# Expert output scattered straight to token order by row numbers carried with the rows, with the second batch's slots behind the first one's return

## The chip, the cores and the metric

The kernel runs on one core of one Trainium2 chip. The metric is the time of one execution on the device, in microseconds (us); lower is better.

## The reference

A network of four residual blocks works on x of shape (2, 1024, 128) in float32. Cut to what matters here:

```python
x = x + attention(layernorm(x))        # 16 heads of 64, both batches
x = x + routed_ffn(layernorm(x))       # the block that the change touches
x = x + ssm(layernorm(x))              # fc1, in_proj, causal conv, selective scan, fc2
x = x + dense_experts(layernorm(x))    # 8 experts, all computed

def routed_ffn(x):                     # 8 experts, 128 -> 512 -> 128
    logits = (x @ wg_red.T) @ wg_unit.T
    e, score = argmax(softmax(logits)), max(softmax(logits))
    h = gelu(x @ w1[e] + b1[e])
    return score * (h @ w2[e] + b2[e])
```

Each token goes to one expert only. The kernel computes the routed block with the tokens sorted by expert.

## The kernel before, in words

One list of steps (`whole_order`, built of `attention_order`, `routed_order`, `first_inputs_order`, `recurrence_order` and `dense_order`) sets the program. Each engine (and SP, which issues most DMAs) walks this list and takes the steps that its own table has; on an engine everything runs in that order, and between engines semaphores set the pace. So a step that waits holds back all later steps of its engine.

**Routing.** A batch has 1024 tokens in 8 tiles of 128. `dve_count` (L1687 on) gives each token a place, so that every expert's tokens begin at a new slot of 128 rows; 15 slots (NSLOT) always do. `pool_scatter` (L2097) writes the 8 tiles of normed rows (`K.xrows`, 128 floats a row) to these places in the HBM tensor `slots_in`, two indirect DMAs to each of four steps. `load_rows` (L1444) loads four slots at once into one of two buffers `slot_rows`; SP issues it for batch 0, ACT for batch 1. Then for each group of four slots PE transposes (`turn`, L770) and ACT copies (`turned`, L1202).

**Slots.** For slot n: SP fetches the expert's weights (`fetch`, 578 KB), PE multiplies (`up`, L783), ACT applies gelu (L1214), PE multiplies again (`down`, L794), DVE adds the bias into one of six buffers `e0_y` (`yrow`, L1732), and SP stores them as slot n of the HBM tensor `slots_out` (L2283). Batch 0 has slots 0 to 14, batch 1 slots 15 to 29 (written s = 15, s + 1, ... below). The first hidden buffers hT share their memory with `slot_rows`.

**Return.** When all 15 slots of a batch are stored, POOL issues 8 gathers (`pool_back`, L2114), each of which brings the 128 rows of one tile in token order. For batch 0, DVE weighs each tile and adds it to x (`return`, L1744 and L1745), then come the layer norm's moments (`lnvar`), POOL's root (`lnroot`, L2031 and L2034) and the normed rows (`lnrows`, L1540), PE's transposes (`lnturn`, L593), and with them the third block: `fc1` (L809), `inp` (L819), 8 convolution taps on DVE (`conv`, L1772 and L1775), silu, `xpj` (L871), `dtp` (L892). For batch 1 the 8 gathers stand beside the units 0 to 7 of the recurrence, ACT weighs (`rescale`, L1178) and PE adds (`readd`, L827 and L829).

**The order around the change.** In `routed_order`, after slot 14 of batch 0: row loads of batch 1, the 8 gathers of batch 0, then batch 1's four `turn`s, the `up`s of s to s + 5 and the `down`s of s to s + 3, while the gathers and the layer norm run; `first_inputs_order` weaves the other slots among the third block's first products.

**Recurrence.** 64 units, each: PE spreads B (L909), DVE multiplies (L1852) and scans (L1859), POOL multiplies with C (L2181), PE adds (L925), ACT makes the decay (L1340).

Of the kernel before, what the change touches and what calls it, by code (L numbers as in the profile page):

```python
# [167 lines left out]
class Names:  # L168
# [7 lines left out]
         (4, 0, 3): [("lnturn", 1, 0), ("lncopy", 1, 0)], (4, 0, 5): [("lnturn", 1, 1), ("lncopy", 1, 1)], (5, 0, 3): [("bias", 1)], (2, 0, 5): [("gdir",)],  # L176
# [147 lines left out]
def routed_order():  # L324


    s, beside = NSLOT, {3: [("lnrows", 3)], 4: turned(3), 8: [("scatter", 1, q) for q in range(4)] + [("fetch", NSLOT)], 10: [("fetch", NSLOT + 1)], 12: [("fetch", NSLOT + 2)]}
# [8 lines left out]
    order += [("rows", 1, 0), ("rows", 1, 1)] + [("back", 0, t) for t in range(NT)] + [("fetch", s + 3)]  # L336
    order += [("turn", 1, 0), ("turned", 1, 0), ("rows", 1, 2), ("fetch", s + 4), ("up", s), ("gelu", s), ("turn", 1, 1), ("turned", 1, 1), ("rows", 1, 3)]
    order += [("up", s + 1), ("gelu", s + 1), ("down", s), ("turn", 1, 2), ("turned", 1, 2)]
    order += [("fetch", s + 5), ("up", s + 2), ("gelu", s + 2), ("down", s + 1), ("turn", 1, 3), ("turned", 1, 3)]
    order += [("up", s + 3), ("gelu", s + 3), ("down", s + 2), ("up", s + 4), ("gelu", s + 4), ("down", s + 3), ("up", s + 5), ("gelu", s + 5)]  # L340
    order += [("return", 0, t) for t in range(5)] + [("yrow", s), ("fetch", s + 6), ("return", 0, 5), ("yrow", s + 1), ("fetch", s + 7)]
    order += [("return", 0, 6), ("return", 0, 7), ("lnvar", 4), ("lnroot", 4), ("yrow", s + 2), ("fetch", s + 8)]
    return order + [("lnrows", 4), ("yrow", s + 3), ("fetch", s + 9)]


def first_inputs_order():

# [415 lines left out]
def pe_turn(K, pe, b, g):  # L763
# [5 lines left out]
    for t in range(n):  # L769
        ins = pe.transpose(bank[:, t * P:(t + 1) * P], R.slot_rows[i % 2][:, t, :], K.ident[:, :])  # L770
# [401 lines left out]
def act_rescale(K, act, t):  # L1172
# [4 lines left out]
    act.wait_ge(K.back[t], 16)  # L1177
# [27 lines left out]
def act_gelu(K, act, n):  # L1205
# [3 lines left out]
    act.wait_ge(R.ld_wts[BUFFER[n]], 16 * (USE[n] + 1))  # L1209
    users = [i for i in range(n) if HIDDEN[i] == HIDDEN[n]]  # L1210
# [233 lines left out]
def load_rows(K, eng, b, g):  # L1444
# [281 lines left out]

def dve_yrow(K, dve, n):
# [8 lines left out]
def dve_return(K, dve, b, t):  # L1736
# [3 lines left out]
    dve.wait_ge(K.back[t], 16)  # L1740
# [219 lines left out]
def dve_added(K, dve, b, c):  # L1960
# [7 lines left out]
    for t in range(4):  # L1968
        tt = 4 * c + t
        xs = K.x[:, b * NT + tt, :]  # L1970
        if last and t == 2:
# [9 lines left out]
             "rate": dve_rate, "count": dve_count, "yrow": dve_yrow, "return": dve_return, "conv": dve_conv, "xpj_take": dve_xpj_take, "xdr": dve_xdr,  # L1981
# [217 lines left out]
POOL_STEPS = {"full": pool_low, "firstroot": pool_first_root, "halfroot": pool_half_root, "xdr": pool_xdr, "dt": pool_dt, "du": pool_du, "centre": pool_centre, "gated": pool_gated, "fc2bias": pool_fc2_bias, "xlo": pool_xlo, "lnroot": pool_root, "e1_root": pool_root1, "score": pool_score, "scatter": pool_scatter, "back": pool_back, "pad": pool_pad,  # L2199
# [12 lines left out]
def sp_first_loads(K, sp):  # L2212
# [24 lines left out]
    for b in range(B):  # L2237
        sp.dma_start(R.slots_in[b].rearrange("(j p) d -> p j d", p=P), R.zero[:, :].unsqueeze(1).broadcast_to([P, NSLOT, D])).then_inc(
# [104 lines left out]
SP_STEPS = {"row": sp_row, "rows": sp_rows, "fetch": sp_fetch, "yrow": sp_yrow, "loads": sp_loads, "e1_load": sp_load_experts,  # L2343
# [11 lines left out]
def two_layer_program(nc, a, out):  # L2355
    K, A, R, X, Y = Names(), Names(), Names(), Names(), Names()
    K.A, K.R, K.X, K.Y, K.a, K.out = A, R, X, Y, a, out
    with ExitStack() as ctx:
# [37 lines left out]
        K.back, K.stored, K.returned, K.scored = sems("row_returned", AT), sem("stored"), sem("returned"), sem("scored")  # L2396
# [210 lines left out]
```

## Time and profile before

| what | value |
|---|---|
| median of 3 runs | 1140.87 us (1140.73 to 1142.6) |
| the profiled execution's own time | 1139.21 us |
| its span | 1137.9 us, 19726 instructions |
| busy: PE, DVE, ACT, POOL | 96%, 73%, 54%, 67% of the span |
| DMA queue of POOL (q0) | 1024 packets, 2.10 MB |

How to read it: the attention takes the time to about 711 us, batch 0's slots to 745 us, the return, batch 1's slots and the third block's first products to 803 us, the recurrence to about 1030 us, and the dense experts the rest. Shares of the whole span say nothing of these stages; the stretch between 733 and 860 us is where the change acts.

### The profile page before, as it was taken

The numbers are of one execution on the slowest core, as the hardware profiler recorded it, in microseconds if no ns is written. First come the engines' busy times: TensorE is split into PE (matmuls) and PEld (weight loads), VectorE is DVE, ScalarE is ACT, GpSimd is POOL, SyncE is SP. The second block draws the span as 40 slices with busy tenths as digits, with TensorE's granted clock in tenths as the row PEclk, the third lists the DMA queues.
The fourth block names the chain that finished last, engine by engine and source line by source line (L and its number), as shares of the span: only waits on it lengthen the run. The fifth ranks groups of instructions, "written<-read, shape, count | busy, mean of one in ns | idle before, by whom it ended". The sixth has DMA issues, their size and how long they took to land.

```text
span 1137.9 us, 19726 instructions
## 1 busy us (share of the span) xinstructions
PE 1088.3 (96%) x7578; PEld 675.5 (59%) x7578; DVE 829.3 (73%) x1226; ACT 618.1 (54%) x866; POOL 761.0 (67%) x394
## 2 busy tenths in 40 slices
PE   7999999999999999999999999969789987899998
PEld 4555665665665665666566566967444434445786
DVE  6875766675775775676876547425889999997987
ACT  5543544553543554554354445546977555757653
POOL 5787788788787797677889850230589796995200
PEclk9999999999999999999999999989899999999999
DMA  6000000000000000000000333475464454440000
GB/s 210 1 3 1 1 2 1 1 2 2 1 2 2 1 1 2 2 1 1 2 11 6 97 113 105 121 233 168 159 204 155 142 164 140 140 158 28 10 10 19
DMA packets 38094, 68.86 MB, mean 61 GB/s; under 512 B 5969, under 2 KB 24145, under 8 KB 38001
## 3 DMA queue, kind: packets, MB, share of 16 engines
q1 hardware_dynamic: 34992, 64.52, 18.0%
q0 software_dynamic: 1024, 2.10, 0.6%
q8 instruction: 61, 1.00, 0.4%
q10 hardware_dynamic: 1984, 0.98, 0.3%
q14 instruction: 33, 0.26, 0.1%
HBM read 61.30 MB, written 6.16 MB: 59 GB/s over the span
## 4 chain that ended last, share of the span: by engine, by line
PE 79%; issue 7%; DVE 5%; POOL 5%; ACT 2%; DMA 1%; POOLq 0%; DVEq 0%; ACTq 0%
PE psum L651 20%; PE psum L612 16%; PE psum L637 6%; PE psum L625 5%; PE psum L669 5%; PE psum L1019 4%; PE psum L925 3%; PE psum L1002 3%; POOL hc L2181 3%; PE psum L717 3%; PE psum L703 3%; PE psum L684 2%; PE psum L794 2%; PE psum L783 1%; DVE psum L1852 1%
## 5 line engine op out<-in xcount | busy, mean ns | idle before, releaser
L2093 POOL TENSOR_TENSOR psums<-psums,prob 128x1024 f32<-128x1024 f32 x180 | 427.7, 2376 | 26.1 <-POOL psums L2093 0.5
L1568 DVE TENSOR_REDUCE mx<-psum 128x2 f32<-128x1024 f32 x256 | 300.8, 1225 | 116.5 <-PE psum L637 116.0
L1118 ACT ACTIVATE prob<-psum 128x1024 f32<-128x1024 f32 x256 | 261.5, 1027 | 64.5 <-PE psum L625 39.8
L651 PE MATMUL psum<-prob,V 128*64 128x512 f32 x1024 | 244.0, 598 | 0.0
L2181 POOL TENSOR_TENSOR hc<-hs,cc 128x1024 f32<-128x1024 f32 x64 | 151.7, 2371 | 21.1 <-DVE hs L1859 18.5
L1859 DVE TENSOR_TENSOR_SCAN hs<-dA,psum 128x1024 f32<-128x1024 f32 x64 | 146.3, 2286 | 2.2
L2093 POOL TENSOR_TENSOR psums<-prob 128x1024 f32<-128x1024 f32 x30 | 72.2, 2406 | 105.3 <-ACT prob L1118 105.3
L1127 ACT COPY oraw<-psum 128x512 f32<-128x512 f32 x32 | 18.8, 588 | 210.8 <-PE psum L651 210.8
L925 PE MATMUL psum<-hc,ident 128*128 128x512 f32 x256 | 122.6, 602 | 2.5 <-DVE slot_rows_h L1867 1.4
L651 PEld LDWEIGHTS psum<-prob,V 128*64 128x64 f32 x1024 | 66.5, 137 | 97.1 <-issue 93.2
L637 PE MATMUL psum<-k_hi,q_hi 64*128 64x512 f32 x512 | 107.7, 410 | 1.7 <-DVE mx L1568 1.3
L612 PE MATMUL psum<-q_hi,k_hi 64*128 64x512 f32 x512 | 106.9, 404 | 0.0
L612 PE MATMUL psum<-q_hi,k_lo 64*128 64x512 f32 x512 | 103.5, 390 | 0.0
L612 PE MATMUL psum<-q_lo,k_hi 64*128 64x512 f32 x512 | 103.3, 390 | 0.0
L625 PE MATMUL psum<-guard,row_one 64*128 64x512 f32 x512 | 103.1, 388 | 0.0
L1627 DVE SCALAR_TENSOR_TENSOR x<-psum,inv,x 128x128 f32<-128x128 f32 x256 | 72.0, 344 | 21.1 <-PE psum L717 15.6
L925 PEld LDWEIGHTS psum<-hc,ident 128*128 128x128 f32 x256 | 48.3, 192 | 44.5 <-issue 32.2
L637 PEld LDWEIGHTS psum<-k_hi,q_hi 64*128 64x128 f32 x512 | 50.3, 184 | 40.3 <-issue 28.0
L909 PE MATMUL psum<-xdr,pickr 128*128 128x512 f32 x128 | 57.1, 528 | 11.9 <-DVE hs L1859 11.6
L612 PEld LDWEIGHTS psum<-q_hi,k_hi 64*128 64x128 f32 x512 | 48.8, 184 | 33.0 <-ACT prob L1118 17.5
L1340 ACT ACTIVATE dA<-slotT,alog 128x1024 f32<-128x1024 f32 x32 | 36.6, 1150 | 40.0 <-DVE hs L1859 39.7
L625 PEld LDWEIGHTS psum<-guard,row_one 64*128 64x128 f32 x512 | 50.8, 184 | 8.7
(294 smaller groups left out, 1709.0 us busy)
## 6 DMA issues: line engine op xcount, KB each, us to landing
cc<-C_rows SPq DMA_DIRECT2D x64, 512.0 KB, 3.7
kq_wts<-in_e_rows SPq DMA_DIRECT2D x14, 578.0 KB, 5.0
e_wts<-in_e_rows SPq DMA_DIRECT2D x10, 578.0 KB, 3.9
e_w<-in_e_rows SPq DMA_DIRECT2D x6, 578.0 KB, 4.3
slots_in<-e_zero SPq DMA_DIRECT2D x2, 960.0 KB, 7.0
slots_out<-e_y SPq DMA_DIRECT2D x30, 64.0 KB, 2.6
e_w<-in_e_w SPq DMA_DIRECT2D x1, 1024.0 KB, 7.5
slot_rows_h<-slots_in SPq DMA_DIRECT2D x3, 256.0 KB, 2.9
```

The costliest lines, as they stand in the source:

```text
L612: pe.matmul(both[:, s, :], left[HALF[s], js], right[HALF[s], cs], start=(part == 0), stop=False)
L625: ins = pe.matmul(both[:, s, :], A.row_one[HALF[s], :], A.guard[q][HALF[s], cs], start=False, stop=True)
L637: ins = pe.matmul(both[:, s, :], A.q_hi[r][HALF[s], t * P:(t + 1) * P], A.k_hi[r][HALF[s], c * CH:(c + 1) * CH], start=True, stop=True)
L651: ins = pe.matmul(A.O[HALF[s], :], A.V[pair % 2][:, j, s * DH:(s + 1) * DH], A.prob[unit(pair, c, j) % NPB][:, s * CH:(s + 1) * CH], start ...
L909: ins = pe.matmul(X.gain[u % 2][:, c * CH:(c + 1) * CH], X.pickr[:, n:n + 1].broadcast_to([P, P]), X.xdr[b][:, c * CH:(c + 1) * CH], start ...
L925: ins = pe.matmul(X.Y[:, c * CH:(c + 1) * CH], K.ident[:, :], X.hc[u % 3][:, c * CH:(c + 1) * CH], start=(u > 0 and n == 0), stop=(n == NS ...
L1118: act.activation(A.prob[n % NPB][:, :], slots.bank("score", pair, c, j).rearrange("p s n -> p (s n)"), ACT.Exp, scale=float(DH) ** -0.5).t ...
L1568: dve.tensor_reduce(K.A.mx[:, :, t, c], slots.bank("max", pair, t, c), AXX, ALU.max).then_inc(*slots.inc("max", pair, t, c))
L1627: ins = dve.scalar_tensor_tensor(out=K.x[:, tile, :], in0=slots.bank("out", pair, c)[:, s, t * P:(t + 1) * P], scalar=A.inv[:, s * NT + 4 ...
L1859: dve.tensor_tensor_scan(X.hs[u % 3][:, :], X.dA[u % 3][:, :], X.gain[u % 2], 0.0, ALU.mult, ALU.add).then_inc(X.state_done, 1)
L2093: pool.tensor_tensor(total[:, :], (K.A.prob[(n - 1) % NPB] if j == 1 else total)[:, :], K.A.prob[n % NPB][:, :], ALU.add).then_inc(*K.psum ...
L2181: pool.tensor_tensor(X.hc[u % 3][:, :], X.hs[u % 3][:, :], X.cc[u % NCC][:, :], ALU.mult).then_inc(X.product_done, 1)
```

## The change

- Every row of `xrows` gets a 129th float. Once, early, DVE writes into it the number at which the token's output row shall stand (`names`): NSLOT * P + token. Two DMAs (`pads`, on SP, beside attention pair 6) write the numbers 0 to 1919 into the 129th column of `slots_in`, for rows that no token takes. So each slot row carries its token's number, and the padding rows carry numbers below 1920.
- DVE copies that column of four loaded slots into an integer tile (`tokens`, one short copy for each group of four slots). A row load waits until the copy of the group that had its buffer before is made.
- The store of a slot on SP goes; POOL scatters the slot's rows to `rows_out` by these numbers (`pool_yrow`): 15 indirect DMAs a batch in place of 8 gathers.
- The gathers go; SP loads the token rows in order, two plain loads of 256 KB a batch (`sp_back`), when all 15 scatters of the batch have landed.
- The order is written anew: batch 0's return, its moments and `lnrows` stand ahead of batch 1's row loads and slots. Batch 1's last scatter step comes behind slot 14. Ahead of `lnturn` of the third block now stand two `turn`s, two `up`s and one `down`; the others come behind.

```diff
-    s, beside = NSLOT, {3: [("lnrows", 3)], 4: turned(3), 8: [("scatter", 1, q) for q in range(4)] + [("fetch", NSLOT)], 10: [("fetch", NSLOT + 1)], 12: [("fetch", NSLOT + 2)]}
+    s, beside = NSLOT, {3: [("lnrows", 3)], 4: turned(3), 8: [("scatter", 1, 0), ("fetch", NSLOT)], 9: [("scatter", 1, 1)], 10: [("fetch", NSLOT + 1)], 12: [("scatter", 1, 2), ("fetch", NSLOT + 2)]}
...
-    order += [("rows", 1, 0), ("rows", 1, 1)] + [("back", 0, t) for t in range(NT)] + [("fetch", s + 3)]
-    order += [("turn", 1, 0), ("turned", 1, 0), ("rows", 1, 2), ("fetch", s + 4), ("up", s), ("gelu", s), ("turn", 1, 1), ("turned", 1, 1), ("rows", 1, 3)]
-    order += [("up", s + 1), ("gelu", s + 1), ("down", s), ("turn", 1, 2), ("turned", 1, 2)]
-    order += [("fetch", s + 5), ("up", s + 2), ("gelu", s + 2), ("down", s + 1), ("turn", 1, 3), ("turned", 1, 3)]
-    order += [("up", s + 3), ("gelu", s + 3), ("down", s + 2), ("up", s + 4), ("gelu", s + 4), ("down", s + 3), ("up", s + 5), ("gelu", s + 5)]
-    order += [("return", 0, t) for t in range(5)] + [("yrow", s), ("fetch", s + 6), ("return", 0, 5), ("yrow", s + 1), ("fetch", s + 7)]
-    order += [("return", 0, 6), ("return", 0, 7), ("lnvar", 4), ("lnroot", 4), ("yrow", s + 2), ("fetch", s + 8)]
-    return order + [("lnrows", 4), ("yrow", s + 3), ("fetch", s + 9)]
+    order += [("scatter", 1, 3), ("back", 0)] + [("return", 0, t) for t in range(NT)] + [("lnvar", 4), ("lnroot", 4), ("lnrows", 4)]
+    order += [("rows", 1, 0), ("rows", 1, 1), ("fetch", s + 3)]
+    order += [("turn", 1, 0), ("turned", 1, 0), ("tokens", 1, 0), ("tokens", 1, 1), ("rows", 1, 2), ("fetch", s + 4), ("up", s), ("gelu", s), ("turn", 1, 1), ("turned", 1, 1), ("rows", 1, 3)]
+    order += [("up", s + 1), ("gelu", s + 1), ("down", s), ("yrow", s)] + turned(4)
+    order += [("turn", 1, 2), ("turned", 1, 2), ("tokens", 1, 2), ("fetch", s + 5), ("up", s + 2), ("gelu", s + 2), ("down", s + 1), ("yrow", s + 1), ("fetch", s + 6)]
+    return order + [("fc1", 0), ("fc1_out", 0), ("turn", 1, 3), ("turned", 1, 3), ("tokens", 1, 3), ("up", s + 3), ("gelu", s + 3), ("down", s + 2), ("yrow", s + 2), ("fetch", s + 7)]
...
+    order = [("inp", 0, 0), ("inp_out", 0, 0), ("up", s + 4), ("gelu", s + 4), ("down", s + 3), ("yrow", s + 3), ("fetch", s + 8)]
+    order += [("inp", 0, 1), ("inp_out", 0, 1), ("up", s + 5), ("gelu", s + 5), ("down", s + 4), ("yrow", s + 4), ("fetch", s + 9)]
     for i in range(4):
         order += [("conv", 0, i // 2, w) for w in (i % 2 * 2, i % 2 * 2 + 1)]
+        order += [("up", s + 6 + i), ("gelu", s + 6 + i), ("down", s + 5 + i), ("yrow", s + 5 + i), ("fetch", s + 10 + i)]
...
-        beside[t] += [("back", 1, t)]
+        beside[t] += [("back", 1)] * (t == 0)
...
 def load_rows(K, eng, b, g):
...
     if i >= 2:
         eng.wait_ge(*K.work.full.at("turn", *divmod(i - 2, 4)))
+        eng.wait_ge(R.tokens, i - 1)
...
+def dve_tokens(K, dve, b, g):
+    R, i = K.R, b * 4 + g
+    n = min(4, NSLOT - 4 * g)
+    dve.wait_ge(R.ld_rows[i % 2], 16 * (i // 2 + 1))
+    dve.tensor_copy(R.tok[b][:, 4 * g:4 * g + n], R.slot_rows[i % 2][:, 0:n, D]).then_inc(R.tokens, 1)
...
+def pool_yrow(K, pool, n):
+    R = K.R
+    b, j = divmod(n, NSLOT)
+    pool.wait_ge(R.tokens, 4 * b + j // 4 + 1)
+    pool.wait_ge(*K.work.empty("down", n))
+    pool.indirect_dma_start(out=R.rows_out[b], out_offset=bass.IndirectOffsetOnAxis(ap=R.tok[b][:, j:j + 1].bitcast(U32), axis=0),
+                            in_=R.yrow[n % NY][:, :], in_offset=None).then_inc(R.y_stored[n % NY], 16)
...
+def sp_pads(K, sp):
+    R = K.R
+    sp.wait_ge(R.named, 1)
+    for b in range(B):
+        sp.dma_start(R.slots_in[b].rearrange("(j p) d -> p j d", p=P)[:, :, D], R.pad[:, :], allow_slow_non_contiguous=True).then_inc(R.padded, 16)
...
+def sp_back(K, sp, b):
+    R = K.R
+    sp.wait_ge(R.scattered[b], 16 * NT)
+    for i in range(NY):
+        sp.wait_ge(R.y_stored[i], 16 * len(range(i, (b + 1) * NSLOT, NY)))
+    for g in range(NC):
+        at = slice(b * NT + 4 * g, b * NT + 4 * g + 4)
+        sp.dma_start(K.xrows[:, at, :], R.rows_out[b][NSLOT * P + g * CH:NSLOT * P + (g + 1) * CH, :].rearrange("(t p) d -> p t d", p=P)).then_inc(K.back[b * NC + g], 16)
```

## Rows read from the trace of the kernel before

**Rows 1.** Busy time of stretches: PE, PEld, DVE, ACT, POOL, then PEclk, DMA share, GB/s

```profile
0.00:570.00 570.00, 564.13 (x4761) 342.99 (x4763) 391.76 (x616) 279.41 (x322) 440.10 (x213) 1.00 0.04 12
...
745.00:769.40 24.40, 13.79 (x96) 12.98 (x95) 7.01 (x33) 9.68 (x30) 9.60 (x10) 0.86 0.76 228
769.40:802.80 33.40, 33.05 (x197) 25.66 (x198) 18.08 (x31) 25.46 (x56) 0.00 (x0) 0.95 0.47 142
808.00:860.00 52.00, 45.62 (x115) 22.14 (x116) 47.43 (x30) 44.20 (x91) 44.34 (x31) 0.91 0.58 194
860.00:1000.00 140.00, 126.86 (x347) 61.31 (x346) 137.86 (x98) 88.05 (x103) 122.91 (x61) 1.00 0.46 147
```

**Rows 2.** Chain that ended last, around batch 0's return: start, length, what

```profile
745.41 3.98 DMA slots_out<-e_y
...
759.11 5.45 DMA xrows<-slots_out,posi
```

**Rows 3.** Timeline of PE: start, length, engine, line, instruction, count, idle before it

```profile
750.23 1.12 PE L770 MATMUL psum<-ident,slot_rows_h 128*128 128x128 f32 x4 [5.18 <-DMA slot_rows_h<-slots_in]
...
757.25 0.60 PE L770 MATMUL psum<-ident,slot_rows_h 128*128 128x128 f32 x4
...
769.44 0.74 PE L593 MATMUL psum<-ident,xrows 128*128 128x128 f32 x4 [3.76 <-DVE xrows L1540]
...
781.02 1.06 PE L794 MATMUL psum<-kq_wts,slot_rows_h 128*128 128x128 f32 x8
781.91 1.06 PE L783 MATMUL psum<-slotT,kq_wts 128*128 128x128 f32 x8
...
802.56 1.42 PE L909 MATMUL psum<-xdr,pickr 128*128 128x512 f32 x4
```

**Rows 4.** Timeline of POOL

```profile
733.35 0.96 POOL L2104 DMA_INDIRECT slots_in<-xrows,posi  x1 [0.30 <-issue]
...
740.93 0.96 POOL L2104 DMA_INDIRECT slots_in<-xrows,posi  x1 [0.30 <-issue]
...
766.56 1.68 POOL L2034 TENSOR_TENSOR rstd<-std,exponent 128x8 f32<-128x8 f32 x1
...
812.05 1.09 POOL L2114 DMA_INDIRECT xrows<-slots_out,posi  x1 [0.17 <-POOL hc L2181]
```

**Rows 5.** Timeline of DVE

```profile
733.06 0.49 DVE L1732 TENSOR_TENSOR e_y<-psum,kq_wts 128x128 f32<-128x128 f32 x2
...
757.45 0.29 DVE L1744 BATCH_NORM_STATS2 stats<-x 128x6 f32<-128x128 f32 x1 [1.03 <-DMA xrows<-slots_out,posi]
...
758.09 0.29 DVE L1744 BATCH_NORM_STATS2 stats<-x 128x6 f32<-128x128 f32 x1
...
764.79 0.34 DVE L1745 SCALAR_TENSOR_TENSOR x<-xrows,score,x 128x128 f32<-128x128 f32 x1
...
768.27 2.13 DVE L1540 TENSOR_SCALAR xrows<-x,mv,rstd 128x128 f32<-128x128 f32 x8 [1.96 <-POOL rstd L2034]
...
779.23 0.81 DVE L1772 TENSOR_SCALAR u<-xc,cw,cb 128x1024 f32<-128x1024 f32 x1 [2.94 <-ACT xc L1232]
...
787.28 2.60 DVE L1775 SCALAR_TENSOR_TENSOR u<-xc,cw,u 128x1024 f32<-128x1024 f32 x2
```

**Rows 6.** DMA issues of the page: KB each, median us from issue to landing

```profile
slot_rows_h<-slots_in SPq DMA_DIRECT2D x3, 256.0 KB, 2.9
slot_rows_h<-slots_in ACTq DMA_DIRECT2D x3, 256.0 KB, 4.3
...
slots_in<-xrows,posi POOLq DMA_INDIRECT x16, 2.2
```

**Rows 7.** Timeline of ACT, one gelu of a slot

```profile
754.15 1.14 ACT L1214 ACTIVATE slot_rows_h<-psum,e_wts 128x128 f32<-128x128 f32 x4 [2.18 <-PE psum L783]
```

**Rows 8.** Who waited for whom, 808 to 860 us: us in total, times, longest

```profile
DVE psum L1852 <- PE psum L909: 4.1, 4, 2.4
...
ACT xrows L1178 <- DMA xrows<-slots_out,posi: 2.8, 2, 1.7
```

More of the change, by code:

```diff
@@ L175 @@
 EARLY = {(3, 0, 3): [("lnvar", 1), ("lnroot", 1)], (3, 1, 3): [("lnrows", 1)],
-         (4, 0, 3): [("lnturn", 1, 0), ("lncopy", 1, 0)], (4, 0, 5): [("lnturn", 1, 1), ("lncopy", 1, 1)], (5, 0, 3): [("bias", 1)], (2, 0, 5): [("gdir",)],
+         (4, 0, 3): [("lnturn", 1, 0), ("lncopy", 1, 0)], (4, 0, 5): [("lnturn", 1, 1), ("lncopy", 1, 1)], (5, 0, 3): [("bias", 1)], (6, 0, 5): [("pads",)], (2, 0, 5): [("gdir",), ("names",)],
          (8, 1, 3): [("lnvar", 2), ("lnroot", 2)], (9, 0, 3): [("lnrows", 2)],
@@ L357, in first_inputs_order @@
-    order += [("xpj", 0), ("xpj_take", 0), ("gelu", s + 11), ("gelu", s + 12), ("pick",), ("up", s + 13), ("up", s + 14), ("dtp", 0, 0), ("xpj_out", 0)]
-    order += [("gelu", s + 13), ("gelu", s + 14), ("xdr", 0), ("dtp_out", 0, 0), ("softexp", 0, 0), ("down", s + 11), ("yrow", s + 11), ("dtp", 0, 1), ("dtp_max",)]
+        order += [("up", s + 6 + i), ("gelu", s + 6 + i), ("down", s + 5 + i), ("yrow", s + 5 + i), ("fetch", s + 10 + i)]
+    order += [("silu", 0, 0), ("up", s + 10), ("down", s + 9), ("silu", 0, 1), ("up", s + 11), ("yrow", s + 9), ("fetch", s + 14)]
@@ L359, in first_inputs_order @@
+    order += [("xpj", 0), ("xpj_take", 0), ("gelu", s + 10), ("gelu", s + 11), ("pick",), ("up", s + 12), ("dtp", 0, 0), ("xpj_out", 0), ("down", s + 10), ("yrow", s + 10)]
+    order += [("up", s + 13), ("gelu", s + 12), ("gelu", s + 13), ("xdr", 0), ("dtp_out", 0, 0), ("down", s + 11), ("yrow", s + 11), ("up", s + 14), ("gelu", s + 14), ("softexp", 0, 0), ("dtp", 0, 1), ("dtp_max",)]
     for n in range(s + 12, s + 15):
@@ L1209, in act_gelu @@
     act.wait_ge(R.ld_wts[BUFFER[n]], 16 * (USE[n] + 1))
+    if HIDDEN[n] < 2:
+        act.wait_ge(R.tokens, 4 * B)
     users = [i for i in range(n) if HIDDEN[i] == HIDDEN[n]]
@@ L1739, in dve_return @@
     t += b * NT
-    dve.wait_ge(K.back[t], 16)
+    dve.wait_ge(K.back[t // 4], 16)
     if t > b * NT:
@@ L1980 @@
              "rowed": dve_row, "valued": dve_values, "sumhalf": dve_sum_half, "out": dve_out, "gsum": dve_gate_squares, "gscale": dve_gate_scale, "gdir": dve_gdir, "choose": dve_choose,
-             "rate": dve_rate, "count": dve_count, "yrow": dve_yrow, "return": dve_return, "conv": dve_conv, "xpj_take": dve_xpj_take, "xdr": dve_xdr,
+             "names": dve_names, "tokens": dve_tokens, "rate": dve_rate, "count": dve_count, "yrow": dve_yrow, "return": dve_return, "conv": dve_conv, "xpj_take": dve_xpj_take, "xdr": dve_xdr,
              "dtp_out": dve_dtp_first, "dtp_max": dve_dtp_max, "dt": dve_dt, "gain0": dve_gain0, "pick": dve_pick, "alog": dve_alog, "unit": dve_unit, "output": dve_output,
@@ L2340, in sp_added @@
     sp.dma_start(K.out.rearrange("(t p) d -> p t d", p=P)[:, at, :], K.x[:, at, :]).then_inc(K.stored, 16)
-SP_STEPS = {"row": sp_row, "rows": sp_rows, "fetch": sp_fetch, "yrow": sp_yrow, "loads": sp_loads, "e1_load": sp_load_experts,
+SP_STEPS = {"row": sp_row, "pads": sp_pads, "rows": sp_rows, "fetch": sp_fetch, "back": sp_back, "loads": sp_loads, "e1_load": sp_load_experts,
             "xpj_out": sp_store_C, "unit": sp_unit, "added": sp_added}
```

65 lines of the change are left out of this document (31 added, 34 removed).

## The prediction

> **What bounds the kernel now.** I first cut the span into stretches by busy time. Between 745.0 and 769.4 us no engine is full: PE works 13.79 of 24.40 us, DVE 7.01, POOL 9.60 [rows 1]. The chain of waits says why: the last slot's store has to land (3.98 us), then 8 gathers follow each other on POOL, and the last one lands 5.45 us after its issue [rows 2]. The timeline of DVE shows the last tile added at 764.79 and the normed rows ready at 768.27 + 2.13 = 770.40; PE's first `lnturn` starts at 769.44 [rows 3, 5]. PE uses this wait for batch 1: four `turn`s, six `up`s and four `down`s stand between 750.2 and 765.7. From there to the recurrence PE is the bound: 33.05 of 33.40 us busy [rows 1], ending with L909 at 802.56 [rows 3]. In the recurrence DVE is: 137.86 of 140 us from 860 on, but only 47.43 of 52 in its first part, 808 to 860 [rows 1]. So time is to be had in two places, the wait of 24 us and DVE's 4.57 idle us; anything added to PE between 769 and 803 us is paid in full.
>
> **Step 1, POOL's queue.** The 15 stores of batch 0 leave SP and become indirect DMAs on POOL, among the 8 scatters of batch 1. Seven scatters in a row start at 733.35 to 740.93, so one takes 7.58 / 6 = 1.26 us of POOL [rows 4]. Slots come every 1.79 us (an `up` and a `down` of 0.89 each, the distance of 781.02 and 781.91 [rows 3]), so slots alone would fit; slots and scatters together don't. DVE finishes slots 6 and 7 between 733.06 and 733.55, together, as it was in the routing sums of batch 1 before [rows 5]. From 733.6 POOL has, in its order: y6, y7, 2 scatters, y8, 2 scatters, y9, y10, y11, 2 scatters, y12, y13, y14. y14 is the 15th, so it starts at 733.6 + 14 x 1.26 = 751.3, although its rows are made at 745.4. Before, the SP store of it started at 745.4.
>
> **Step 2, the return.** A scatter lands 2.2 us after its issue begins [rows 6]: 753.5. SP then issues two loads of 256 KB. The same size and row length took 2.9 us from SP in a quiet stretch and 4.3 us from ACT in a busy one [rows 6]. No weight fetch runs beside these two (the next one waits for PE's `turn`), so I take 2.9 and 0.2 for the issue: first tile at 756.6. DVE takes 0.64 us a tile where it does not wait (757.45 to 758.09 [rows 5]), so the eighth is added from 756.8 + 7 x 0.64 = 761.3, against 764.79: 3.5 us earlier. From there to the last normed row it was 770.40 - 764.79 = 5.6 us, moments, POOL's root (1.68 us [rows 4]) and `lnrows`, and no scatter is left on POOL then (the last two start at 752.6 and 753.8). New end of `lnrows`: 766.9.
>
> The Trainium skill (DMA: Bandwidth & Descriptors, "Anatomy of one DMA — SWDGE (gpsimd) path") gives 2.0 us plus bytes over 436 GB/s, an estimate of 2.6 us for 256 KB; by it the return would be 0.3 us earlier than by my row.
>
> **Step 3, a new wait on ACT.** ACT's load of rows (1,2) now waits for `tokens` (1,0). In the list that copy stands on DVE behind `lnrows`, and behind the load on ACT stands gelu s; PE's `down` s waits for gelu s, and `lnturn` is queued behind `down` s. So after 766.9: the copy (0.3 at most, a 128 x 128 add is 0.25 each [rows 5]), gelu 1.14 [rows 7], `down` 0.89, hand-overs 0.3: 769.5. At half clock `down` takes 0.9 more: 770.4. I take 769.9, which is 0.5 us **later** than the 769.44 of before, though the rows came back 3.5 us earlier. Batch 1's row loads (issued at about 756.2, landing by 760.5 at 4.3 us) are ready long before and decide nothing.
>
> **Step 4, work moved behind.** Ahead of `lnturn` PE now does two `turn`s, two `up`s, one `down`; before, four, six and four. Behind it come 4 `up`s and 3 `down`s more, 7 x 0.89 = 6.2 us, and two `turn`s, 0.60 (four slots [rows 3]) and some 0.48 (three): 7.3 us. PE has 0.35 us free in the stretch [rows 1], so nothing hides it: +7.3. The half clock at the stretch's start (0.95 mean [rows 1]) stays about as it is.
>
> **Step 5, the convolution.** The taps with four bias adds between them took DVE from 779.23 to 787.28 + 2.60 = 789.88, 10.65 us [rows 5]. They now stand behind `yrow` s + 4, so behind `down` s + 4, at about 785.3, and end at about 795.9; PE has work until about 795.2 by the sum so far, and `xpj` needs the second half of the silus some 1.8 us into itself. Late by 0 to 1 us; I take +0.3.
>
> **Step 6, the recurrence.** Eight gathers leave POOL (1.09 us and a gap of 0.17 beside each product [rows 4]), and ACT no longer waits 2.8 us for them [rows 8]. DVE waited for PE's L909 4.1 us in four places [rows 8]; each follows from `readd`, a silu or a transposition which ACT or POOL made late. I take all 4.1 back; bounds are 0 (PE and ACT in order keep them) and 4.57. After 860 DVE is full, so this gain stays. The second batch's `back` lands behind unit 0 and is first needed at unit 2.
>
> **Costed at nothing.** `names` and four `tokens` beside the attention: some 0.3 us each on a DVE with 391.76 of 570 us busy [rows 1]. SP loses its stores and gets `back`, behind which the fetches of s + 3 and on queue; they wait for `turn`s anyway and their slots come later than before. The six `e0_y` buffers: a scatter issued at 739.9 or so has landed when slot 14 needs its buffer; if not, DVE and PE would stop some 1 us. POOL's last three scatters of batch 1 end at about 812.5, its first `du` is then due at 813.5: cover 1 us. `pads`: DMA share there is 0.04 [rows 1]; uncovered it would hold SP's guard rows of one pair. The Trainium skill (same page, "Rules for kernel authors") says that a non-contiguous last dimension becomes one descriptor per element, so 2 x 1920; no row here shows such a transfer. Rows of 129 floats in place of 128 are 0.8% more bytes; at worst a row load is later by 1.4 us, the distance of the two kinds of load [rows 6], and those loads decide nothing.
>
> **Sum.** +0.5 + 7.3 + 0.3 - 4.1 = **+4.0 us**. The profiled execution took 1139.21 us (span 1137.9), so its like would be 1143.2; the median of the runs is 1.66 above it: 1140.87 + 4.0 = **1144.9 us**.
>
> **Rivals.**
> - *The return is early enough, not slower.* If POOL's descriptors overlapped its gaps so that y14 went out when made, at 745.7, steps 2 and 3 would come 5.6 us earlier: 4.0 - 5.6 = -1.6, 1139.3. It decides as soon as one indirect DMA costs POOL under about 0.9 us. Against it: seven at 1.26 without exception [rows 4]. With it, and DVE's last 0.5 idle us back too, 1138.8. A milder one: half of that, 1142.
> - *The recurrence gives nothing back.* ACT is busy 44.20 of 52 us there and reloads tables, PE 45.62 [rows 1]; if the four waits stay, +8.1: 1149.0. For it: only 2.8 us are waits for gathers. Against it: each wait lies behind one of them.
> - *TensorE cold for longer.* The granted clock was 0.86 over the wait [rows 1]: after 5.18 idle us the same transposes took 1.12 us, at 757.25 only 0.60 [rows 3], the two levels of 1.2 and 2.4 GHz. Now PE idles from 745 to 760 and works in pieces to 770. If it stays at the lower level for 4 us more from 770 on, half of them is lost: +6.0, 1146.9. The Trainium skill (TensorE: Matmul & The Clock Gate, "Part 1") says that the half-rate state is the default and activity releases it; the trace agrees.
> - *The burst of fetches.* Behind `turn` (1,2) ten fetches go out at once, and scatters share the DMA engines (0.76 busy in the wait already [rows 1]): if y scatters and row loads land 2 us later each, +2 to +4, 1147 to 1149.
> - *`pads` stalls attention*: one guard row late by 5.45 us, the slowest landing shown [rows 2]: 1150.3.
>
> **How the numbers follow.** Two runs of this kernel differ by about 0.2%, 2.3 us: faster is under 1138.6, slower over 1143.2. Forecast as worked out (+2.3 to +6): 0.48. Early return 0.18, of which 0.10 passes under 1138.6; step 3 or 4 shorter than summed (0 to +2.3) 0.16; nothing given back 0.05, cold clock 0.06, burst 0.05, pads 0.02. Faster 0.10, same 0.08 + 0.16 = 0.24, slower 0.48 + 0.18 = 0.66. Range 1139.8 to 1149.5.
>
> **What would show it.** Right: y14's scatter starts near 751; last return near 761; gelu s right behind the `tokens` copy, near 767; `lnturn` near 770; L909 of unit 0 near 810.5 (802.56 before); DVE's waits for L909 under 1 us up to unit 12. Wrong: y14 before 748, `lnturn` before 766, or PE idle behind `lnturn`.

## The result and the profile after

The changed kernel took 1146.73 us (median of 7 runs, 1146.28 to 1148.21) against 1142.6 us of the kernel before in the same session (7 runs, 1140.73 to 1145.37): a ratio of 1.0039, 95% interval 1.0027 to 1.0052, so 3.1 to 5.9 us slower. The forecast was slower by 4.0 us.

The profiled execution after took 1146.28 us, its span was 1144.9. Its busy time by stretch (columns as in [rows 1]):

```profile
745.00:769.40 24.40, 8.79 (x44) 8.04 (x45) 6.27 (x28) 4.48 (x15) 9.97 (x11) 0.64 0.27 74
769.40:810.00 40.60, 38.34 (x254) 31.27 (x253) 17.24 (x36) 28.45 (x75) 12.28 (x12) 0.96 0.60 211
810.00:860.00 50.00, 41.85 (x130) 21.52 (x129) 47.66 (x37) 47.65 (x89) 35.87 (x21) 0.93 0.58 199
```

PE worked 8.79 us of the wait for batch 0's rows, where it had worked 13.79 [rows 1]. Some of the 8.79 is batch 0's last slots, late in this execution; in the second profile below PE works 6.35 us of the same stretch. What the prediction doesn't have stands in the chain that ended last, before that wait:

```profile
735.83 0.91 PE psum L791 x8
736.80 7.62 another core or an unknown queue
744.47 2.88 another core or an unknown queue
...
755.74 2.24 DMA rows_out<-e_y,e_wg
758.16 3.74 DMA xrows<-rows_out
```

PE, ACT and DVE stood still in turn between 737 and 754 us (called "the stop" below), and no instruction that the profile shows released them; POOL went on issuing an indirect DMA every 1.26 us until 743.27. Slot 14's rows were made at 754.69, 9.3 us later than in the next profile when both are counted from the same event, and its scatter began at 755.74, not at 751.3. One profile can't say whether the change does this, so the kernel was profiled again (run look_after, under "The experiments"), and the second profile shows nothing of it. It is the one to read the steps from. Line numbers are those of each kernel's own file: `turn`, `up`, `down`, `lnturn`, `fc1` and the spread of B, L770, L783, L794, L593, L809 and L909 before, are L767, L780, L791, L590, L806 and L906 here.

POOL, DVE, ACT and PE of this second profile (span 1142.9, 1144.18 us), in four views (timelines, columns as in [rows 3 to 5]); first POOL:

```profile
734.79 0.96 POOL L2134 DMA_INDIRECT rows_out<-e_y,e_wg  x1 [4.75 <-DVE e_y L1750]
...
752.50 0.96 POOL L2134 DMA_INDIRECT rows_out<-e_y,e_wg  x1 [0.30 <-issue]
```

That is y6 and y14, with 13 indirect DMAs between them: 17.71 / 14 = 1.265 us each, although slot 14's rows were made 6.7 us before their turn:

```profile
745.77 0.29 DVE L1750 TENSOR_TENSOR e_y<-psum,e_wts 128x128 f32<-128x128 f32 x1 [1.21 <-PE psum L791]
758.74 0.35 DVE L1763 SCALAR_TENSOR_TENSOR x<-xrows,score,x 128x128 f32<-128x128 f32 x1 [12.67 <-DMA xrows<-rows_out]
...
763.31 0.34 DVE L1763 SCALAR_TENSOR_TENSOR x<-xrows,score,x 128x128 f32<-128x128 f32 x1
...
766.77 2.14 DVE L1540 TENSOR_SCALAR xrows<-x,mv,rstd 128x128 f32<-128x128 f32 x8 [2.13 <-POOL rstd L2052]
768.83 0.23 DVE L1742 CAST e_wg<-slot_rows_h 128x4 int32<-128x4 f32 x2
```

The rows are all added at 763.31 instead of 764.79 [rows 5]; the last line is the two `tokens` copies, 0.23 us together, right behind `lnrows`. ACT, whose gelu s waits behind the row load that needs these copies:

```profile
769.59 0.63 ACT L1213 ACTIVATE slot_rows_h<-psum,e_wts 128x128 f32<-128x128 f32 x2 [5.29 <-DVE e_wg L1742]
```

PE, where `down` s (L791) waits for this gelu, and `lnturn` (L590) and `turn` (1,2) (L767) stand behind `down` s:

```profile
766.24 1.06 PE L767 MATMUL psum<-ident,slot_rows_h 128*128 128x128 f32 x4
767.09 1.80 PE L780 MATMUL psum<-slotT,e_wts 128*128 128x128 f32 x8
770.79 1.16 PE L791 MATMUL psum<-e_wts,slot_rows_h 128*128 128x128 f32 x8 [1.89 <-ACT slot_rows_h L1213]
771.78 1.64 PE L590 MATMUL psum<-ident,xrows 128*128 128x128 f32 x8
773.21 1.07 PE L767 MATMUL psum<-ident,slot_rows_h 128*128 128x128 f32 x4
```

The granted clock was at its lower level (0.50) up to 768.6, while PE had worked since 762.57, and at its upper level (1.00) from 768.7 to 772.0, so `down` s took only 0.99 us to the next start. Behind the gap of 1.89 us it was at 0.50 again from 772.1 to 775.4: `turn` (1,2) took 1.07 us, like the `turn` at 766.24.

And who waited for whom between 808 and 860 us, where DVE had waited 4.1 us for L909 [rows 8]:

```profile
DVE psum L1870 <- PE psum L906: 0.3, 1, 0.3
```

### The profile page after: what moved, and what is told of

It is laid out like the page before. It is cut to its first block, busy times and chain, and to the rows that moved or that the text cites. A ratio compares the mean times of both kernels' runs of the same rounds, so it can differ in the third digit from the quotient of the medians.

```text
span 1144.9 us, 19769 instructions
## 1 busy us (share of the span) xinstructions
PE 1088.9 (95%) x7578; PEld 676.0 (59%) x7578; DVE 836.1 (73%) x1237; ACT 617.7 (54%) x866; POOL 775.3 (68%) x408
## 4 chain that ended last, share of the span: by engine, by line
PE 74%; issue 9%; DVE 7%; ACT 4%; POOL 3%; DMA 1%; another core or an unknown queue 1%; SPq 0%; DVEq 0%; POOLq 0%; ACTq 0%
PE psum L648 20%; PE psum L609 16%; PE psum L634 6%; PE psum L622 5%; PE psum L666 5%; PE psum L1016 3%; PE psum L999 3%; DVE psum L1870 3%; PE psum L714 3%; PE psum L700 2%; PE psum L681 2%; POOL hc L2201 2%; PE psum L791 2%; PE psum L780 2%; DVE hs L1877 2%
## 5 line engine op out<-in xcount | busy, mean ns | idle before, releaser
L906 PE MATMUL psum<-xdr,pickr 128*128 128x512 f32 x128 | 56.0, 519 | 11.4 <-DVE hs L1877 11.2
L2134 POOL DMA_INDIRECT rows_out<-e_y,e_wg x30 | 30.1, 1004 | 48.8 <-DVE e_y L1750 40.3
```

## Fourteen profiles cut at the same five places

One table carries most of what follows. Each execution is cut where an event is easy to find in every kernel: PE's first transposition of the second block's rows (**a**, just after the attention), the first `lnturn` behind batch 0's return (**b**), and the start of the scans of unit 0, unit 14 and the last unit on DVE (**c**, **d**, **e**). Times in us; "before" is the median, column by column, of five profiles (spans 1137.1, 1137.2, 1137.8, 1137.9, 1140.1).

| kernel | a | a to b | b to c | c to d | d to e | e to end | span |
|---|---|---|---|---|---|---|---|
| before, 5 profiles | 718.29 | 50.62 | 37.72 | 53.15 | 174.41 | 103.13 | 1137.8 |
| after, first profile | 718.71 | 56.32 | 43.75 | 49.02 | 173.98 | 103.12 | 1144.9 |
| after, look_after | 719.07 | 52.71 | 44.95 | 49.00 | 173.97 | 103.20 | 1142.9 |
| after, look_after2 | 719.00 | 53.37 | 45.37 | 48.99 | 173.96 | 103.21 | 1143.9 |
| tokens_first | 718.70 | 50.60 | 43.29 | 49.00 | 173.96 | 103.15 | 1138.7 |
| scatters_last | 720.03 | 51.19 | 43.29 | 49.00 | 173.97 | 103.12 | 1140.6 |
| order_alone | 719.92 | 49.39 | 47.57 | 51.82 | 174.78 | 103.12 | 1146.6 |
| mech_alone | 719.68 | 53.92 | 36.25 | 48.99 | 173.96 | 103.20 | 1136.0 |
| hybrid | 720.00 | 50.62 | 37.70 | 48.99 | 173.97 | 103.22 | 1134.5 |
| hybrid_again | 718.32 | 51.38 | 37.69 | 49.00 | 173.97 | 103.14 | 1133.5 |

Between before and look_after: +0.8 up to a, +2.1 to b, +7.2 to c, -4.15 to d, -0.4 to e. The columns from c on hardly scatter between executions of one kernel (in the five of before by 0.4 us at most). Those ahead of c do: a by 2 us over all fourteen, a to b by 1.5 and b to c by 1.1 us in the five of before. The timed runs of before scatter by 2.6 to 7.0 us within a session.

## The experiments

**Is the stop part of the change?** Both kernels unchanged, profiled again.

> The kernel before, unchanged, looked at once more. The profiled run of it took 1139.21 us, less than any of its timed runs (1140.7 to 1145.4). Theory A (the stop of all engines together between 737 and 754 us in the profile after comes from outside the program, now and then, in either kernel): this look shows 1139 to 1146 us, and where it is longer than 1139.2 a stop in which PE, ACT and DVE all end a wait at once stands somewhere. Theory B (the stop belongs to the change): no such stop, and a run within 1 us of 1139.2.

> The kernel after, unchanged. In its first profile slots 10 to 14 were made at 744.4 to 754.7 us behind a stop of all engines, where 738 to 745.1 was due, and slot 14's scatter began at 755.7 and not at 751.3. Theory A (the stop comes from outside the program): the stop is gone or elsewhere, slot 14's scatter begins at 751 to 752, first lnturn at 770.5 to 771.5, recurrence unit 0 at 812 to 814, time 1142 to 1144 us. Theory B (the change causes it): the stop is there again at 737 to 754 us, with lnturn at 774 to 776 and a time of 1145.5 to 1148 us.

look_before: 1141.41 us, no stop; its extra 2 to 3 us lie in the return (a to b 52.03) and behind it (b to c 38.67), so theory A was wrong to expect a stop there, and the time isn't within 1 us of 1139.2, as theory B had it. look_after: 1144.18 us, slot 14's scatter at 752.50, `lnturn` at 771.78, no stop: theory A, each number up to 0.5 us later than it gave. A third profile of the changed kernel:

> The changed kernel, a third look. If the stop between 737 and 754 us came from outside: again none, slot 14's scatter 33.4 us behind the transposition of the second block's rows, lnturn 52.7 behind it, 49.0 us from unit 0's scan to unit 14's. If the stop belongs to the change: lnturn 55 us and more behind.

It took 1145.18 us, without a stop: rows of slot 14 made at 745.70, first row returned at 758.48, `lnturn` 53.37 behind a, 0.7 more than expected. The stop stands in one of three profiles of the changed kernel and in none of five of the kernel before. That excludes a stop which the change always brings, not one that it brings now and then; its cause stays open.

How many of the timed runs of the first comparison held a stop isn't known: of the seven of the changed kernel, the profiled one with the stop, 1146.28 us, is the shortest. The kernel before took longer in that session too (median 1142.6) than in the later ones (1138.7 to 1140.1). The executions without a stop took 1144.18 us against a median of 1139.98 of before beside it, and 1145.18 against 1138.43, 1138.46 and 1140.13: 4.2 to 6.8 us more. So the change is slower without a stop as well.

**Step 3, the tokens ahead of `lnrows`.**

```diff
-    order += [("scatter", 1, 3), ("back", 0)] + [("return", 0, t) for t in range(NT)] + [("lnvar", 4), ("lnroot", 4), ("lnrows", 4)]
+    order += [("scatter", 1, 3), ("back", 0)] + [("return", 0, t) for t in range(NT)] + [("lnvar", 4), ("lnroot", 4)]
...
-    order += [("turn", 1, 0), ("turned", 1, 0), ("tokens", 1, 0), ("tokens", 1, 1), ("rows", 1, 2), ("fetch", s + 4), ("up", s), ("gelu", s), ("turn", 1, 1), ("turned", 1, 1), ("rows", 1, 3)]
+    order += [("turn", 1, 0), ("turned", 1, 0), ("tokens", 1, 0), ("tokens", 1, 1), ("lnrows", 4), ("rows", 1, 2), ("fetch", s + 4), ("up", s), ("gelu", s), ("turn", 1, 1), ("turned", 1, 1), ("rows", 1, 3)]
```

> The changed kernel with the two copies of batch 1's token numbers ahead of the normed rows on DVE. Theory (step 3 of the prediction: ACT's load of rows waits for these copies, gelu s and PE's down s behind it): gelu s starts at 767 to 769 us instead of 772.84, down s ends ahead of the normed rows, lnturn starts 0.2 us behind them instead of 2.87, 2.2 to 2.8 us less than the changed kernel: ratio to before 1.001 to 1.002. Rival (PE had to do gelu s and down s somewhere, and what it does ahead of lnturn only takes other work's place, or the clock falls again): less than 0.8 us less than the changed kernel, ratio 1.003 to 1.004.

1140.09 us against 1139.98 of before (ratio 1.0001, 0.999 to 1.0012): the 4 us of the change are gone, more than the theory's 2.2 to 2.8, and the ratio is better than its 1.001 to 1.002. `lnturn` stood 0.95 us behind the last normed row (768.35), not 0.2, since `down` s was still running. PE in its trace (`down` s, `lnturn`, `turn` (1,2)):

```profile
768.15 1.31 PE L791 MATMUL psum<-e_wts,slot_rows_h 128*128 128x128 f32 x8
769.30 1.04 PE L590 MATMUL psum<-ident,xrows 128*128 128x128 f32 x8
770.17 0.60 PE L767 MATMUL psum<-ident,slot_rows_h 128*128 128x128 f32 x4
```

`lnturn` is 2.48 us earlier than in look_after, 2.1 of it counted from a: the wait. The other gain is the clock: PE works on without the gap of 1.89 us, and the granted clock, which is at 1.00 from 768.7 on as in look_after, stays there, so that the same `turn` takes 0.60 us and not 1.07. From `lnturn` to unit 0 it is 43.29 instead of 44.95 us, 1.66 less for the same work, and all of it ahead of `fc1` (3.09 instead of 4.75 us). So the wait on ACT cost twice, as time and as clock.

**Steps 1 and 2, batch 1's scatters behind slot 14's.**

```diff
-    s, beside = NSLOT, {3: [("lnrows", 3)], 4: turned(3), 8: [("scatter", 1, 0), ("fetch", NSLOT)], 9: [("scatter", 1, 1)], 10: [("fetch", NSLOT + 1)], 12: [("scatter", 1, 2), ("fetch", NSLOT + 2)]}
+    s, beside = NSLOT, {3: [("lnrows", 3)], 4: turned(3), 8: [("fetch", NSLOT)], 10: [("fetch", NSLOT + 1)], 12: [("fetch", NSLOT + 2)]}
...
-    order += [("scatter", 1, 3), ("back", 0)] + [("return", 0, t) for t in range(NT)] + [("lnvar", 4), ("lnroot", 4), ("lnrows", 4)]
+    order += [("scatter", 1, q) for q in range(4)] + [("back", 0)] + [("return", 0, t) for t in range(NT)] + [("lnvar", 4), ("lnroot", 4), ("lnrows", 4)]
```

> The changed kernel with the eight scatters of batch 1's rows all behind slot 14's own scatter on POOL. Theory (steps 1 and 2: POOL's queue at 1.26 us per indirect DMA delays slot 14): slot 14's scatter starts within 1.3 us of its rows being made (745.7 us without a stop), first row returned at 751 to 753, last normed rows at 761 to 763, lnturn at 764 to 766, 5 to 6 us less than the changed kernel: ratio to before 0.998 to 1.000. Rival (batch 1's rows, loaded only once they are scattered, now come last: eight scatters from 747 to 757, landed at 759.3, load landed at 763 to 764, transposition, up, gelu and down s and the normed transpositions behind them): lnturn at 768 to 770, only 1 to 3 us less than the changed kernel, ratio 1.001 to 1.003. If the scatter of slots costs nothing extra beside the return: no difference.

1140.32 us (ratio 1.0002, 0.9991 to 1.0014), between the two ranges and nearer to the theory's. Slot 14's scatter, DVE's first row and the end of the return, from two timelines of this kernel:

```profile
747.78 0.96 POOL L2134 DMA_INDIRECT rows_out<-e_y,e_wg  x1 [0.54 <-issue]
```

```profile
746.73 0.29 DVE L1750 TENSOR_TENSOR e_y<-psum,e_wts 128x128 f32<-128x128 f32 x1 [1.20 <-PE psum L791]
753.98 0.35 DVE L1763 SCALAR_TENSOR_TENSOR x<-xrows,score,x 128x128 f32<-128x128 f32 x1 [6.95 <-DMA xrows<-rows_out]
...
762.00 2.14 DVE L1540 TENSOR_SCALAR xrows<-x,mv,rstd 128x128 f32<-128x128 f32 x8 [2.12 <-POOL rstd L2052]
```

The scatter waits 1.05 us instead of 6.7 and the rows are normed at 764.14, 4.8 us earlier than in look_after. But `lnturn` starts at 771.22. The chain of this kernel shows what holds it now:

```profile
758.06 2.31 DMA slots_in<-xrows,posi
...
760.39 2.85 DMA slot_rows_h<-slots_in
...
763.28 1.12 PE psum L767 x4
...
765.12 2.05 PE psum L780 x8
```

The last of batch 1's scatters, their landing and load, and two `turn`s, two `up`s and a `down` that stand ahead of `lnturn` in PE's order: the rival, to the mechanism. Its price was set too low (1 to 3 us less), since here too PE works without a gap and the granted clock is back at its upper level with `lnturn` (b to c 43.29). POOL's 23 indirect DMAs of this stage are 29 us of its time at 1.265 each, whatever stands first, and PE needs both kinds.

**Half of the change each.**

The order alone, against the kernel before (its later lines as in the change):

```diff
-    order += [("rows", 1, 0), ("rows", 1, 1)] + [("back", 0, t) for t in range(NT)] + [("fetch", s + 3)]
+    order += [("scatter", 1, 3)]+ [("back", 0, t) for t in range(NT)] + [("return", 0, t) for t in range(NT)] + [("lnvar", 4), ("lnroot", 4), ("lnrows", 4)]
+    order += [("rows", 1, 0), ("rows", 1, 1), ("fetch", s + 3)]
```

The new way alone, against the changed kernel (its later lines as before the change):

```diff
-    order += [("scatter", 1, 3), ("back", 0)] + [("return", 0, t) for t in range(NT)] + [("lnvar", 4), ("lnroot", 4), ("lnrows", 4)]
-    order += [("rows", 1, 0), ("rows", 1, 1), ("fetch", s + 3)]
-    order += [("turn", 1, 0), ("turned", 1, 0), ("tokens", 1, 0), ("tokens", 1, 1), ("rows", 1, 2), ("fetch", s + 4), ("up", s), ("gelu", s), ("turn", 1, 1), ("turned", 1, 1), ("rows", 1, 3)]
+    order += [("rows", 1, 0), ("rows", 1, 1)] + [("fetch", s + 3)]
+    order += [("turn", 1, 0), ("turned", 1, 0), ("tokens", 1, 0), ("tokens", 1, 1), ("rows", 1, 2), ("fetch", s + 4), ("back", 0), ("up", s), ("gelu", s), ("turn", 1, 1), ("turned", 1, 1), ("rows", 1, 3)]
```

> The kernel before (slots stored by SP, eight gathers on POOL) with the changed kernel's order of batch 1's first work: four ups, two downs' worth and two turns behind the normed rows, batch 1's last scatters ahead of the gathers. Theory (steps 4 and 6 of the prediction: the order alone costs PE its cover of 24 us, and the gain in the recurrence comes from the gathers going): PE idle from 747 to about 763 us, the first lnturn no earlier than 769, everything behind it 5 to 8 us later at recurrence unit 0, DVE's waits for L909 between 808 and 860 still above 2 us: ratio to before 1.004 to 1.007. Rival (the recurrence gains because fewer ups and gelus stand in it or they come in a better order, not because the gathers are gone): the waits fall below 1 us here too, ratio 1.001 to 1.003.

1146.73 us against 1138.9 of before: ratio 1.0072 (1.0056 to 1.0087), at the top of what was expected and a little over it. DVE's waits for PE from 804 to 862 us did not go, although c to d is 1.3 us shorter than before's:

```profile
DVE psum L1849 <- PE psum L906: 3.0, 2, 2.3
```

Behind `lnturn` it lost 2.65 us more than look_after up to L906 (42.72 against 40.07): 0.90 by a colder clock up to `fc1` and 1.64 by weights, which PE didn't wait for in look_after. The longer of the two:

```profile
795.02 1.16 PE L780 MATMUL psum<-slotT,e_w 128*128 128x128 f32 x8 [1.33 <-DMA e_w<-in_e_rows]
```

SP's slot stores stand ahead of its fetches here and wait for each slot: it issued the weights of this `up` at 789.70. In look_after, without the stores, its fetches were all issued by 786, and PE didn't wait for weights. This relief the prediction had not counted.

> The changed kernel's way of bringing the rows back (scatters on POOL when made, two loads) with the order of the kernel before: batch 1's first turns, ups and downs while batch 0's rows return. Theory (the new way gives 4 us in the recurrence and up to 3 us of an earlier return, the order takes 7 away): PE works through the wait again, lnturn at 766 to 769 us, recurrence unit 0 within 2 us of before's, its waits for PE still under 1 us: ratio to before 0.994 to 0.998. Rival 1 (POOL's queue makes batch 1's scatters and slot 14's scatter late for both: batch 1's rows land only at 760 and PE's cover can't be used, the return loads wait behind transfers): lnturn at 770 or later and ratio 0.999 to 1.003. Rival 2 (the gain in the recurrence belongs to the new order): waits of 2 us and more come back, ratio 0.998 to 1.001.

1137.17 us, ratio 0.9983 (0.9974 to 0.9992): faster than before, by less than the theory's 0.994 to 0.998 and more than rival 1's 0.999 to 1.003. `lnturn` came at 773.60, where rival 1 had it: all eight scatters of batch 1 stand ahead of the last slots, DVE waited 5.17 us for one of the six buffers before it could make slot 14's rows (750.35), and y14's scatter began at 755.60. With batch 1's `yrow`s behind the return on DVE even PE stopped:

```profile
767.29 1.61 PE L794 MATMUL psum<-kq_wts,slot_rows_h 128*128 128x128 f32 x8 [4.70 <-DVE e_y L1753]
```

It wins all the same, by c to e (-4.6) and by b to c (36.25 against 37.72): PE worked until 0.87 us ahead of `lnturn`, and the granted clock was 1.00 from 771.2 on. Against that stand 3.3 us more from a to b.

**Only what pays.** The kernel before with batch 1 alone on the new way: batch 0's slots still stored by SP and gathered, batch 1's scattered and loaded, all in the order of before. Against the changed kernel, in POOL's `yrow` and in the order (SP keeps its own `yrow` for batch 0):

```diff
     b, j = divmod(n, NSLOT)
+    if b == 0:
+        return
...
-    order += [("scatter", 1, 3), ("back", 0)] + [("return", 0, t) for t in range(NT)] + [("lnvar", 4), ("lnroot", 4), ("lnrows", 4)]
+    order += [("rows", 1, 0), ("rows", 1, 1)] + [("gather", 0, t) for t in range(NT)] + [("fetch", s + 3)]
```

> Batch 0 as in the kernel before (stored by SP, eight gathers), batch 1 as in the changed kernel (scattered by POOL when made, two loads), all in the order of the kernel before. Theory (what the change gives is the eight gathers gone from the recurrence, and that alone needs neither the new order nor the scatters of batch 0): everything up to 800 us as before within 0.5 us, DVE's waits for PE between 808 and 860 under 1 us, 3 to 4.5 us less than before: ratio 0.996 to 0.9975. Rival (y scatters of slots s+5 to s+14 on POOL in the stretch from 770 to 812 delay slots, or the waits belong to the order): ratio 0.998 to 1.001.

1136.21 us, ratio 0.9978 (0.9969 to 0.9987), the fastest so far, though 2.7 us and not the 3 to 4.5 expected. The stages are as expected: b to c as before (37.70), c to e 4.6 us shorter. But a came at 720.0, and its granted clock shows why (first 25 us; this kernel, then look_before2):

```profile
0.00:25.00 25.00, 20.17 (x85) 9.84 (x85) 16.09 (x40) 13.21 (x21) 13.75 (x26) 0.93 0.98 233
```

```profile
0.00:25.00 25.00, 19.15 (x111) 10.12 (x113) 16.52 (x42) 13.96 (x22) 15.49 (x28) 1.00 0.81 238
```

> The kernel before, looked at a third time. Its timed runs reach from 1136.1 to 1143.1 us, while both profiles of it stand at 1139.2 and 1141.4. In the profiles so far the moment at which PE transposes the second block's rows (718.0 to 720.0 us) differs by 2 us between executions, and the mean granted clock of the first 100 us was 0.98 instead of 1.00 where it was late. Theory: everything in this kernel that varies lies in these two places: the clock's rise in the first 100 us (up to 2 us) and how often DVE waits for L909 between 808 and 860 us (3 to 5 us). Rival: the return of the rows, by gathers, varies too: the first lnturn comes 51.4 and 52.0 us behind that moment in the two profiles, and here by more than 1.5 us off both.

> The kernel before, a fourth look, with what is said for the third: lnturn 51 to 52.5 us behind the transposition of the second block's rows, 49 + 4 to 4.6 us from unit 0's scan to unit 14's.

1138.43 and 1138.46 us: from a to b 50.62 in both, a little under the range; from c to d 53.12 and 53.14, at the low end. So the recurrence hardly varies, and the return does, between 50.6 and 52.0, as the rival had it, but by less than its 1.5 us.

> The kernel before once more, on the chip of the run beside it. The mixed kernel was 2.6 us faster than before in its timed runs, but 4.5 us shorter than the fastest profile of before when both are counted from PE's transposition of the second block's rows. The difference of 2 us lies ahead of that moment: 720.0 us in its profile, at a granted clock of 0.93 in the first 25 us, against 718.0 to 718.4 at 1.00 in four profiles of before. If that early clock is chance of an execution: here 718.3 or 719.9, either way. If it belongs to the chip: the same in both kernels of this call.

> The mixed kernel once more. If the late start (720.0 us, early clock 0.93) is chance of an execution or of the chip: it can stand at 718.3 here, and the timed runs then show up to 4.5 us less than before, ratio 0.996 to 0.9975. If it belongs to this kernel: again 720.0, timed again 2 to 3 us less than before, ratio 0.9975 to 0.9985. In both cases 49.0 us from unit 0's scan to unit 14's.

look_before4: 1139.08 us, a at 718.44. hybrid_again: 1135.4 us, ratio 0.9969 (0.9957 to 0.9981), a at 718.32 with the early clock at 1.00. The late start isn't the kernel's: it stands in four executions, on two chips, and is gone here in the same kernel. The mixed kernel is 3.3 us faster than before in these timed runs, and the span of its profile 4.3 us shorter than that of look_before4 beside it. The intervals of the two comparisons overlap, so they don't say by themselves that the late start made the difference.

## Why the prediction was right

It forecast +4.0 us and slower; measured were +3.1 to +5.9. The mechanism held in every step that the traces can show, but step 3 was given +0.5 us and measured +2.1, so that the nearness of the medians' +4.1 is partly luck. The signs it named came in look_after as: y14's scatter at 752.50 (forecast 751), gelu s at 769.59 (767), `lnturn` at 771.78 (770), the spread of B for unit 0 at 811.85 (810.5), with a itself 1.05 us later than in the profile that the forecast was read from. By its steps, from look_after:

- **Step 1** held: 1.265 us per indirect DMA against 1.26. y14 started at 752.50, 33.43 behind a; forecast 751.3 was 33.28 behind the a of that profile.
- **Step 2** was 0.9 us short. The row load took 3.73 us in the chain of look_after, 3.74 in the first profile, not 2.9; the first row came 0.9 late, counted from a, and the eight took 0.65 each as forecast. I had taken the quiet load of [rows 6]; the measured one is between the two rows. The Trainium skill's fit (DMA: Bandwidth & Descriptors, "Anatomy of one DMA — SWDGE (gpsimd) path"), an estimate of 2.6 us, lies further off. It was made for DMAs that GpSimd issues, and this load is issued by SP, so it should not have been used here; the measurement decides.
- **Step 3** is the mis-sized term. It held in its mechanism: gelu s starts 0.68 us behind the end of `lnrows` at 768.91 with a wait of 5.29 us for the copy, and `lnturn` 2.87 us behind that end (forecast 3.0). In size it was 2.1 us against before's median, not 0.5: 0.9 from step 2, and 0.8 because the profile of before that I read had its `lnturn` 0.8 us later than the median of five.
- **Step 4** held: two kernels with PE working up to `lnturn`, in the new and the old order, need 43.29 and 36.25 us to unit 0, so the moved work costs 7.04 us (forecast 7.3). "The clock stays as it is" was roughly so: the stretch at the lower clock behind `lnturn` costs 1.66 us in look_after (44.95 - 43.29) and about 1.4 before (37.64 of look_before2 - 36.25).
- **Step 5** held: the taps ended at about 797.6 in the timeline of DVE, PE's `xpj` began at 797.40 with a gap of some 0.2 us before it.
- **Step 6** held: 53.15 to 49.00 is -4.15 (forecast -4.1), and DVE's waits for PE fell from 4.1 to 0.3. That it is the gathers and not the order, order_alone shows (51.82, and 174.78 behind it); mech_alone and hybrid get all of it in the old order. Another 0.44 us behind unit 14 had not been counted.

Of the rivals, early return fell with 1.265 us per DMA, and "nothing given back" with the 4.15 us. The burst of fetches held nothing up: from `lnturn` to the spread of B for unit 0, PE waited for no DMA in look_after. "TensorE cold for longer" hardly showed there: the granted clock was 0.50 from 772.1 to 775.4, in the profile of before from 769.9 to 773.2, and the difference is 0.3 us. In look_after2 it was 0.50 until 776.6, 4.3 us behind `lnturn`, and b to c was 0.4 us longer again. The rival's price of 2 us was not reached. Where the clock is lost, it is where a wait left PE idle just ahead of `lnturn`; the Trainium skill's rule (TensorE: Matmul & The Clock Gate, "Part 1") that activity releases the half rate agrees with the `turn` of 1.07 and 0.60 us. `pads` didn't stop attention. PE did wait once for a guard row in each of the three profiles of the changed kernel, 0.5 to 0.8 us, but at about 28 us, long before `pads`, and a is 0.4 to 0.8 us later in them. tokens_first has the same code up to there and doesn't wait, and its a is 0.4 us later too; why is not shown.

From the table the sum for look_after is +0.8 (up to a) +2.1 +7.2 -4.15 -0.4 = +5.6, where the forecast had +0.5 +7.6 -4.1. The spans of the two profiles without a stop are 5 to 6 us longer than before's median span. That is more than the medians' 4.1, whose interval reaches 5.9; the kernel before was slow in the session of those medians.

## What to carry to other kernels

A change that pays in one stage may carry an order that it doesn't need: here the gain (4.6 us in the recurrence) came from taking eight gathers off POOL, and the loss from giving up PE's work beside the return (7 us) and from a copy in the wrong place. The other half, 15 more indirect DMAs at 1.265 us on POOL, brought nothing ahead of `lnturn`: in tokens_first, without the misplaced copies, a to b was as long as before (50.60 against 50.62), and in mech_alone, where both batches wait for POOL's queue, 3.3 us longer. Do each half alone before judging the whole; the mixed kernel, 3.3 us faster than before, came from that. And read what stands between a late copy and the engine that needs it: two copies, 0.23 us together, stood behind `lnrows`, and moving them ahead gave 4 us.

## What had not been expected of the hardware

- In these kernels a wait ahead of PE's work cost clock besides its own length. From `lnturn` to `fc1`, the same work took 3.09 us in tokens_first, where PE had no gap, 4.75 in look_after behind a gap of 1.89 us, 5.18 in look_after2 behind 1.69, and 5.65 in order_alone behind 10.57. So the loss was 1.7 to 2.6 us and didn't grow in step with the gap.
- The first 25 us ran at a granted clock of 0.93 in hybrid, mech_alone, order_alone and scatters_last and at 1.00 in the others, and a is 1.4 to 1.7 us later in them than in before's median. The last of these ran on another chip than the first three, beside runs without it. It makes profiles of single executions differ by more than many changes do; cutting them at common events takes it out.
- One of the fourteen profiles held a stop of PE, ACT and DVE, which made slot 14's rows 9.3 us late; the two others of the same kernel did not have it. Its cause is not known. The scatter behind it was only 3.6 us late, since POOL's queue stood ahead of it anyway.
